# Routed experts block by block, their shares multiplied into y, and the output formed by accumulating transfers

## What is computed

```python
x = x + xattn(_layernorm(x), ctx_1024, Wq, bq, Wk, bk)     # x: (4, 256, 256)
x = x + ffn(_layernorm(x), gate_w, w_gate, w_up, w_down, sh_gate, sh_up, sh_down, se_gate_w)

# xattn: softmax((ctx Wq^T + bq)(ctx Wk^T + bk)^T), applied over the sequence to the normalised x
# ffn, for 1024 tokens, 8 experts, top 2:
scores = xf @ gate_w.T
ew, ei = jax.lax.top_k(scores, 2)
ew = jax.nn.softmax(ew, axis=-1)
x1 = jax.nn.silu(jnp.einsum('td,ehd->teh', xf, w_gate))    # hidden width 128
x3 = jnp.einsum('td,ehd->teh', xf, w_up)
expert_out = jnp.einsum('teh,edh->ted', x1 * x3, w_down)
routed = jnp.einsum('te,ted->td', comb, expert_out)        # comb: ew on the two chosen experts
shared = jax.nn.silu(xf @ sh_gate.T) * (xf @ sh_up.T) @ sh_down.T
sgate = jax.nn.sigmoid(xf @ se_gate_w.T)
return routed + sgate * shared
```

## Time and profile before

| What | Value |
|---|---|
| median of 3 runs | 107.85 us (105.22 to 108.12) |
| the profiled execution's own time | 105.32 us |
| its span, first to last instruction | 103.5 us |
| PE busy | 85.5 us, 83% |
| DVE busy | 62.1 us, 60% |
| ACT busy | 46.5 us, 45% |
| POOL busy | 44.8 us, 43% |
| moved by transfers | 17.50 MB, mean 169 GB/s |

### The profile page before, as it was taken

The page is one execution under the profiler, slowest core; times in us unless marked ns, Lnnn a source line. Parts: engine busy times, 40 slices in busy tenths (PEclk is TensorE's granted clock), DMA queues, the critical chain, the costliest instruction groups (busy, mean ns, idle before and its releaser), DMA issues.

```text
span 103.5 us, 1864 instructions
## 1 busy us (share of the span) xinstructions
PE 85.5 (83%) x514; PEld 68.5 (66%) x514; DVE 62.1 (60%) x274; ACT 46.5 (45%) x104; POOL 44.8 (43%) x60
## 2 busy tenths in 40 slices
PE   6799999997999999996799999999999989600000
PEld 2386789895974478443789999999999968400000
DVE  1188989999999889202986444566444320604990
ACT  0556657758685991433036454466454361000000
POOL 7012002388676777300000567668667677710000
PEclk9999999999999999999999999999999999985555
DMA  2975999992232222256163434655412212059946
GB/s 20 376 267 133 410 413 401 333 348 77 93 108 104 104 104 104 104 142 177 26 186 104 112 107 134 188 152 161 154 46 100 96 56 101 0 90 355 369 180 225
DMA packets 10586, 17.50 MB, mean 169 GB/s; under 512 B 1613, under 2 KB 6095, under 8 KB 10576
## 3 DMA queue, kind: packets, MB, share of 16 engines
q1 hardware_dynamic: 7264, 10.63, 32.7%
q0 software_dynamic: 1872, 4.27, 11.2%
q10 hardware_dynamic: 1440, 2.49, 6.6%
HBM read 10.85 MB, written 7.44 MB: 177 GB/s over the span
## 4 chain that ended last, share of the span: by engine, by line
PE 64%; DMA 12%; DVE 12%; issue 3%; DVEq 3%; POOLq 1%; POOL 1%; ACT 1%; ACTq 0%
PE bank L1064 20%; PE bank L998 12%; PE bank L1079 9%; DMA upper_y<-routed_dram 6%; PE bank L1048 4%; DMA proj_sb<-proj 4%; PE bank L942 4%; PE bank L1034 4%; PE bank L898 3%; PE bank L923 3%; DVEq L285 2%; DMA routed_dram<-y_sb,place 2%; PE bank L906 2%; DVE x L642 2%; PE bank L907 2%
## 5 line engine op out<-in xcount | busy, mean ns | idle before, releaser
L365 POOL DMA_INDIRECT routed_dram<-y_sb,place x23 | 23.6, 1025 | 25.0 <-DVE place L780 15.4
L1064 PEld LDWEIGHTS bank<-xgT,hidden_w 128*128 128x128 f32 x184 | 22.4, 192 | 2.3 <-issue 1.8
L1064 PE MATMUL bank<-xgT,hidden_w 128*128 128x128 f32 x184 | 22.6, 275 | 1.1 <-DVE hidden_w L798 1.1
L352 POOL DMA_INDIRECT slots_dram<-rows,slot x16 | 15.7, 981 | 6.8 <-issue 4.4
L998 PE MATMUL bank<-xnT,ffn_sb 128*128 128x512 f32 (+1 forms) x36 | 14.6, 550 | 0.0
L806 DVE TENSOR_TENSOR r_act<-bank,r_silu 128x256 f32<-128x256 f32 (+1 forms) x12 | 5.0, 414 | 15.9 <-ACT r_silu L514 14.2
L1079 PE MATMUL bank<-ffn_sb,r_act 128*128 x46 | 12.0, 382 | 0.3 <-ACT y_sb L526 0.3
L514 ACT ACTIVATE r_silu<-bank 128x256 f32<-128x256 f32 (+1 forms) x12 | 4.5, 376 | 15.3 <-PE bank L1064 15.3
L998 PEld LDWEIGHTS bank<-xnT,ffn_sb 128*128 128x128 f32 x36 | 6.6, 190 | 5.5 <-issue 5.3
L798 DVE COPY hidden_w<-ffn_sb 128x512 f32 x23 | 8.7, 419 | 1.9 <-issue 1.9
L1079 PEld LDWEIGHTS bank<-ffn_sb,r_act 128*128 128x128 f32 x46 | 7.8, 190 | 1.2 <-issue 0.7
(11 more groups left out here) (119 smaller groups left out, 128.9 us busy)
## 6 DMA issues: line engine op xcount, KB each, us to landing
ffn_sb<-ffn SPq DMA_DIRECT2D x2, 1536.0 KB, 9.6
xg<-slots_dram SPq DMA_DIRECT2D x23, 132.0 KB, 2.2
slots_dram<-empty SPq DMA_DIRECT2D x1, 1056.0 KB, 14.2
x_sb<-x ACTq DMA_DIRECT2D x4, 256.0 KB, 5.0
ffn_sb<-ffn SPq DMA_DIRECT2D x1, 768.0 KB, 4.3
lower_y<-routed_dram SPq DMA_DIRECT2D x2, 256.0 KB, 4.2
lower_y<-routed_dram ACTq DMA_DIRECT2D x2, 256.0 KB, 4.5
upper_y<-routed_dram SPq DMA_DIRECT2D x2, 256.0 KB, 5.6
```

Of the source, the lines that this page charges most:

```text
L352: pool.indirect_dma_start(out=slots_dram[:, :], out_offset=bass.IndirectOffsetOnAxis(ap=slot[:, i, a:a + 1], axis=0), in_=rows[:, i, :], i ...
L365: pool.indirect_dma_start(out=routed_dram[0:planes * TOKENS, :], out_offset=bass.IndirectOffsetOnAxis(ap=place[:, j:j + 1], axis=0), in_=y ...
L1064: last = pe.matmul(hidden_of(p, kind)[:, j % 2, :], hidden_w[:, j % NW, c:c + P], xgT[:, p % 2, k, j % 2, :], start=(k == 0), stop=(k == K ...
```

## The change

The routed stage goes over the 23 blocks one by one: every function takes a block number j, each buffer holds one block, and each semaphore counts blocks. The banks of PSUM are dealt out anew. In DVE's list `experts()` and the first weight copies stand ahead of `shared_act(1, 0)`; in PE's list `shared_up(1, 0)` stands ahead of `shared_gate(1, 1)`.

Two more columns of a table row carry the token's first expert (L + 2) and its negated, scaled margin (L + 3); DVE writes them in `slots`. In the routed stage a DVE instruction makes +-0.5 from the expert (`half`), ACT takes the tanh of the margin column (`lean_of`), DVE makes the share (`share_of`), and ACT's copy of y multiplies by it (`store_y`). `routed_dram`, `lower_y`, `upper_y`, `add_lower`/`add_upper` on DVE and the stores by SP and ACT go. POOL's scatters write to the output tensor itself, which has a second plane for the lower experts' rows. At the end POOL issues four accumulating transfers that add the lower plane to `x1`, then four that add `x1` to the upper plane in DRAM; the first of each wait for the scatters that they need and for `base(1)`.

```diff
-NY = 3
+NY = 6
-LOWS = 4
-UPS = 4
+PARTS = 4
...
-        SH_OUT = [[bank[6], bank[3]], [bank[7], bank[2]]]
+        SH_OUT = [[bank[6], bank[3]], [bank[1], bank[3]]]
         XG_BANK = [bank[0], bank[7]]
-        GU_BANK = [bank[1], bank[2]]
-        Y_BANK = [bank[6], bank[3]]
+        GU_BANK = [bank[4], bank[5]]
+        Y_BANK = [bank[6], bank[2]]
...
             for j in range(BLOCKS):
                 if j >= NXG:
-                    sp.wait_ge(xgT_ready, (j - NXG) // 2 + 1)
-                    sp.wait_ge(place_ready, (j - NXG) // 2 + 1)
+                    sp.wait_ge(xgT_ready, j - NXG + 1)
+                    sp.wait_ge(place_ready, j - NXG + 1)
+                    sp.wait_ge(lean_ready, j - NXG + 1)
                 sp.dma_start(xg[:, j % NXG, :], slots_dram[bass.ds(first[j], P), :]).then_inc(xg_in[j % NXG], 16)
...
             def send_y(j):
...
+                pool.wait_ge(y_stored, j + 1)
+                pool.wait_ge(place_ready, j + 1)
                 planes = 1 if j == LAST else 2
                 pool.indirect_dma_start(
-                    out=routed_dram[0:planes * TOKENS, :],
...
+                    out=planes_of[0:planes * TOKENS, :],
...
+            def add_lower(k):
+
+                t = tiles_of(k)
+                pool.dma_start(x1[:, t, :], out_tiles(1, t), accum_op=ALU.add).then_inc(lower_added[k], 16)
+
+            def add_to_out(k):
+
+                t = tiles_of(k)
+                pool.wait_ge(lower_added[k], 16)
+                pool.dma_start(out_tiles(0, t), x1[:, t, :], accum_op=ALU.add).then_inc(out_stored, 16)
...
             for j in range(BLOCKS):
                 send_y(j)
+            for i in range(NY):
+                mine = [j for j in range(LAST) if j % NY == i]
+                pool.wait_ge(y_sent[i], 16 * len(mine))
+            pool.wait_ge(base_ready, HALVES)
+            for k in range(PARTS):
+                add_lower(k)
+            pool.wait_ge(y_sent[LAST % NY], 16 * rows_sent(LAST % NY))
+            for k in range(PARTS):
+                add_to_out(k)
...
+            def store_y(j):
+                act.wait_ge(y_ready, j + 1)
+                if j >= NY:
+                    act.wait_ge(y_sent[j % NY], 16 * (j // NY))
+                act.wait_ge(share_ready, j + 1)
+                act.activation(y_sb[:, j % NY, :], y_of(j), ACT.Copy, scale=share[:, j:j + 1]).then_inc(y_stored, 1)
+
+            def lean_of(j):
+                act.wait_ge(half_ready, j + 1)
+                act.activation(lean[:, j:j + 1], xg[:, j % NXG, L + 3:L + 4], ACT.Tanh,
+                               scale=half[:, j:j + 1]).then_inc(lean_ready, 1)
...
+            for j in range(BLOCKS):
+                routed_silu(j)
+                if j + 2 < BLOCKS:
+                    store_xgT(j + 2)
+                lean_of(j)
+                if j >= 1:
+                    store_y(j - 1)
+            store_y(BLOCKS - 1)
...
             def slots(b):
                 both = slice(b * LT, (b + 1) * LT)
+
+                dve.tensor_copy(rows[:, both, L + 2], topi[:, both, 0])
+                for i in range(b * LT, (b + 1) * LT):
+                    dve.scalar_tensor_tensor(rows[:, i, L + 3:L + 4], top[:, i, 1:2], top[:, i, 0:1], rstd2[:, i:i + 1],
+                                             ALU.subtract, ALU.mult)
                 dve.wait_ge(prefix_ready, b + 1)
...
+            def places(j):
+
+                dve.wait_ge(xg_in[j % NXG], 16 * (j // NXG + 1))
+                dve.tensor_scalar(plane[:, j:j + 1], xg[:, j % NXG, L + 1:L + 2], expert[:, j:j + 1], float(TOKENS),
+                                  ALU.is_equal, ALU.mult).then_inc(plane_ready, 1)
+
+                dve.tensor_scalar(half[:, j:j + 1], xg[:, j % NXG, L + 2:L + 3], expert[:, j:j + 1], 0.5,
+                                  ALU.not_equal, ALU.subtract).then_inc(half_ready, 1)
+                dve.wait_ge(plane_ready, j + 1)
+                dve.tensor_tensor(place[:, j:j + 1], plane[:, j:j + 1], xg[:, j % NXG, L:L + 1].bitcast(I32),
+                                  ALU.add).then_inc(place_ready, 1)
+
+            def share_of(j):
+                dve.wait_ge(lean_ready, j + 1)
+                dve.tensor_scalar(share[:, j:j + 1], lean[:, j:j + 1], 0.5, 0.5, ALU.mult,
+                                  ALU.add).then_inc(share_ready, 1)
...
             base(0)
-            shared_act(1, 0)
             experts()
             stage(0)
+            stage(1)
+            shared_act(1, 0)
+            stage(2)
             places(0)
...
+            for j in range(BLOCKS):
+                routed_act(j)
+                if j + 3 < BLOCKS:
+                    stage(j + 3)
+                if j == 0:
+                    shared_act(1, 1)
+                share_of(j)
+                if j + 1 < BLOCKS:
+                    places(j + 1)
             base(1)
-            dve.wait_ge(base_ready, 2)
-            for i in range(NT):
-                add_lower(i)
-            for i in range(NT):
-                add_upper(i)
...
             shared_gate(1, 0)
+            shared_up(1, 0)
             shared_gate(1, 1)
-            shared_up(1, 0)
...
+            for j in range(BLOCKS):
+                routed_hidden(j)
+                if j + 2 < BLOCKS:
+                    gather_T(j + 2)
+                if j == 0:
+                    shared_up(1, 1, [1])
                 else:
-                    routed_down(p - 1)
-            routed_down(PAIRS - 1)
+                    routed_down(j - 1)
+            routed_down(BLOCKS - 1)
             shared_down(1, 0)
             shared_down(1, 1)
```

More of the change, by code:

```diff
@@ L46, with xattn_moe_kernel @@
 AX = mybir.AxisListType
[L49 removed]
+def xattn_moe_kernel(nc, proj, x, ffn, slots_dram, out):
     with ExitStack() as ctx:
@@ L131, in xattn_moe_kernel @@
         plane = sb("plane", [P, JB])
+        half = sb("half", [P, JB])
+        lean = sb("lean", [P, JB])
+        share = sb("share", [P, JB])
         place = sb("place", [P, JB], I32)
@@ L150, in xattn_moe_kernel @@
         xg_in = [sem(f"xg_in{i}") for i in range(NXG)]
-        lower_in = [sem(f"lower_in{i}") for i in range(LOWS)]
-        upper_in = [sem(f"upper_in{i}") for i in range(UPS)]
-        lower_added = sem("lower_added")
+        lower_added = [sem(f"lower_added{i}") for i in range(PARTS)]
         warm_ready, ident_ready, const_ready = sem("warm_ready"), sem("ident_ready"), sem("const_ready")
@@ L244, in rows_sent @@
+        def y_of(j):
+            return Y_BANK[j % 2][:, 0:L]
         def rows_sent(i):
-            return sum(blocks_in(p) for p in range(PAIRS) if p % NY == i)
+            return sum(1 for j in range(BLOCKS) if j % NY == i)
         LAST = BLOCKS - 1
[L252 to L272, removed]
@@ L516, in store_y, with store_xgT @@
-            def store_y(p):
-                if p >= NY:
-                    mine = [q for q in range(p) if q % NY == p % NY]
-                    act.wait_ge(y_sent[p % NY], 16 * sum(blocks_in(q) for q in mine))
-                if p < SINGLE:
-                    act.wait_ge(y_ready, 2 * p + 2)
-                    act.copy(y_sb[:, p % NY, :, :], tiles(Y_BANK[p % 2])).then_inc(y_stored, 2)
-                else:
-                    for j in range(2 * p, 2 * p + blocks_in(p)):
-                        act.wait_ge(y_ready, j + 1)
-                        act.copy(y_sb[:, p % NY, j % 2, :], y_of(j)).then_inc(y_stored, 1)
+            def store_xgT(j):
+                act.wait_ge(xgT_ready, j + 1)
+                if j >= 2:
+                    act.wait_ge(gu_ready, j - 1)
+                act.copy(xgT[:, j % 2], XG_BANK[j % 2][:, 0:KT * P].rearrange(
+                    "p (k n) -> p k n", k=KT)).then_inc(xgT_stored, 1)
@@ L1086, in _, with routed_down @@
+            def routed_down(j):
+                if j < 2:
+                    pe.wait_ge(base_ready, 1)
+                else:
+                    pe.wait_ge(y_stored, j - 1)
+                pe.wait_ge(r_act_ready, j + 1)
+                u = bass.ds(chosen[j], 1)
+                pe.matmul(y_of(j), r_act[:, j % 2, :], ffn_sb[:, u, 2 * L:3 * L].rearrange("p o n -> p (o n)"),
+                          start=True, stop=True).then_inc(y_ready, 1)
             pe.wait_ge(warm_ready, 1)
```

238 lines of the change are left out of this document (58 added, 180 removed).

## The result

The changed kernel takes 110.81 us (median of 4 runs, 110.03 to 112.48), the kernel before in the same comparison 106.55 us (median of 4, 105.22 to 108.12): a ratio of 1.051, 95% interval 1.044 to 1.058. The ratio takes only the executions in the faster of the two states in which one and the same kernel can run, 110.03, 110.72 and 110.91 us against 105.22 and 105.25. The forecast was 106.3 us, 1.4% faster than before; the measured time lies within the stated range (102.6 to 111.5), but on the other side of no change, so the forecast was wrong.

What follows compares the result with a forecast made beforehand. PE was taken to bound the routed stage. `base(1)` at 88.7, first issue 89.46, seven more at 1.29 and a landing of 3.5 gave 102.0 against 103.5, so 106.3 us on the median; range 102.6 to 111.5.

Steps and rivals of the forecast that it cites:

- Start of the routed stage: Ahead of the first hidden matmul: the earlier register load and weight copies bring it 1.8 us forward, bounds 0 and 2.1.
- batch 0's stand on the chain, the others' are off it: New DVE instructions in `slots(b)`: 0.25 us for each batch, but only the first batch's lie on the chain of waits.
- Inside the stage: Routed blocks: PE stays at 1.545 us a block, ACT at most 1.45, DVE 1.44; the queue of scatters goes.
- The hand-overs rival: Routed stage: another 0.15 us a round on ACT or DVE makes 3.5 us, in all 110; chance 0.08.
- The tail: After `base(1)`: eight accumulating POOL transfers from 89.46, the eighth issued at 98.5, the end at 102.0, 1.5 us less.
- POOL's pace decides: Transfers at the end: POOL's 1.29 us per issue, not release by landings, sets the eighth issue at 98.5.
- Landing in 3.5, bounds 2.9 to 4.5: Transfers at the end: 2.5 us as for a scatter, plus about 1 us for 256 KB more of reading.
- a sign of being wrong: Transfers at the end: landing needs much over 4.4 us, so that each phase waits for the other's data.
- The rule set against the change: Transfers at the end: adding runs at half a copy's rate, about 10.5 us for 2 MB, an end near 102.
- POOL's queue becomes the bound: Transfers at the end: twice the descriptors, 2.28 us per issue, 5.4 us more, 113.4; chance 0.17.
- Cheap issue: Transfers at the end: POOL issues 0.8 us apart, the second term costs nothing, 5.1 us less, 102.7; chance 0.18.
- The tables: ACT in the routed stage: tanh evicts silu's table, two loads a block, some 50 us more; chance 0.01.

Runs made afterwards that it cites:

- the pair without pauses: Profiles on one chip of the kernel before (105.23 us) and of a3_plain_tail (102.83 us).
- f_no_columns: The changed kernel without DVE's writes of the two new columns, so all shares are a half: 117.71 us, 1.054 of before.
- the run with more slack: a3_plain_tail with the product for y two rounds behind instead of one and a third buffer for `r_act`: 103.71 us, 0.982 of before.
- a3_plain_tail: The changed kernel with the loads by SP and ACT, DVE's adds and the stores of before: 102.83 us against 105.69, ratio 0.974.
- c_copies_on_pool: The changed kernel with POOL's eight accumulating transfers as plain copies, without the adding: 113.14 us, 1.016 of before.

## Why the prediction was wrong, step by step

**Start of the routed stage: right in kind, two thirds of the size.** Forecast was 1.8 us net; it came 49.85 - (51.20 - 2.54) = 1.2 us earlier, and 1.4 in the pair without pauses. The register load does follow `base(0)`, and PE's wait ahead of the first hidden matmul fell from 1.13 us to 0.24. The step that was mis-sized is "batch 0's stand on the chain, the others' are off it": the chain shows 0.08 + 0.25 = 0.33 us in each of three batches, 1.0 us where 0.25 was allowed, and `f_no_columns` confirms it for two of them. In the pair without pauses the shared expert's 16 matmuls ahead of the stage start 37.95 - 37.18 = 0.77 us later, 0.5 more than the 0.25 allowed, which is about what is missing (0.4 to 0.6).

**Inside the stage: right.** Rounds of 1.54 us; scatters no longer queued, the last at 89.55 - 2.54 = 87.0 (86.62 in the pair; forecast 85.7, with 0.4 to 0.6 of the difference from the start). The followers fit: y's copy with the share takes 0.467 us (bound 0.59), the tanh 0.296 (forecast 0.21), with silu 0.278 and xgT's copy 0.373 in all 1.41 for 1.45. Stage by blocks 36.91 us, by pairs 36.27: 0.44 of the 0.64 are two blocks' transposes, which by pairs stood ahead of the stage, and PE's idle time is 0.46 instead of 0.29. That is why the end of `base(1)` moved by only 90.49 - (92.49 - 2.54) = 0.54 us, not 1.8: 1.2 from the start less 0.64. The hand-overs rival did not come; DVE was busy for 22.5 us in the stage, 0.98 a block, where the forecast had up to 1.44.

**The tail: wrong, and the whole of the loss.** The steps that failed are the landing of an accumulating transfer among others and the drain at the end, which the sum did not have. In us behind the end of `base(1)`:

| | Forecast | Measured |
|---|---|---|
| first issue | 0.8 | 0.7 |
| eighth issue | 9.8 | 10.3 |
| last landing | 13.3 | 16.0 |
| end of the program | 13.3 | 18.2 |

The eighth issue came out right for a wrong reason. "POOL's pace decides" failed: an issue costs 0.85 to 0.96 us, not 1.29, and the issues of the second half wait for landings. "Landing in 3.5, bounds 2.9 to 4.5" failed next: the last took 5.76. It priced the adding by what a transfer alone adds to a scatter, and that is nearly right for one alone (3.9 measured), but eight went through full engines at 160 to 198 GB/s. The forecast had named this as a sign of being wrong, a landing of much over 4.4 us with each phase waiting for the other's data, and so it came. The third failure is no term in the sum at all: the program ends with POOL's drain, 2.2 us after the last landing with the final semaphores.

Against the forecast the end lies 6.15 us too late (108.15 for 102.0): 1.25 are the end of `base(1)`, 0.45 the eighth issue, 2.25 its landing and 2.2 the drain. Against before the sum closes too: the end of `base(1)` 0.54 us earlier, the tail 18.20 - 13.04 = 5.16 longer, 4.6 us in all; the spans differ by 108.15 - 103.53 = 4.6. Of the tail, 6.05 us are the adding (by the run without it, 12.15), so that without it the tail would have been 0.9 shorter than the 13.04 before.

**The rule set against the change** held in these profiles. The engines needed 2.1 times as long for the adding transfers as for copies of the same bytes; half of 410 GB/s is 205, and the full engines moved 160 to 198. This is the Trainium skill's "Collectives: The Full Stack" (The bandwidth ceiling), where an adding transfer runs at half a copy's rate. The estimate from it gave an end near 102 from a first issue at 89.46. From the measured one, 93.14, it would give 105.7 for the last landing, which came at 108.5, as the engines moved less at either end (145 GB/s from 95 to 97 us, 162 from 105 to 107). The drain is not in it. That it comes from a second read through one ring, the reason that the Trainium skill gives, no run here shows.

**The rivals.** "POOL's queue becomes the bound" had the right side and its mechanism was refuted: the issue distance that it needed was over 1.51 us, and issues took 0.9. Cheap issue was right in its distance, 0.8, and wrong that the second term costs nothing. The tables were not evicted: tanh beside silu in every round took 0.296 us.

**What stays open.** What POOL's drain waits for is not known. On the two chips with pauses the stage by blocks took 40.1 to 43.4 us in seven profiles, by pairs 36.7, 38.0, 38.0 and 41.3. Whether blocks, with less slack per hand-over, suffer more from a pause, or these profiles caught more of them, was not settled: the run with more slack went where there are none. It matters for the version with the old tail, which gains 2.6% on one chip, while on the two others it can't be told from before (0.995 and 0.997).

## What to carry to other kernels

Before a final add is moved into accumulating transfers, price it at half a copy's rate with several in flight, against the adds of an idle engine: here (`a3_plain_tail`) DVE did the 16 adds in 5.5 us beside loads at twice the rate. Look at who issues the program's last transfer; if it is POOL, add 2 us. Split a change that has several parts before judging it: the finer blocks, the shares in y and the new order are worth 2.6% together where nothing pauses, which the tail more than ate.

## What the runs showed of the hardware

- An accumulating transfer of 256 KB lands 3.9 us after its issue when alone, and in 5.4 to 6.4 us (medians) with others in flight; the engines are then full at 160 to 198 GB/s, beside 410 for plain loads. Eight of them occupied all 16 engines for 13.0 us, plain copies of the same bytes for 6.1.
- POOL issues such a transfer in 0.85 to 0.96 us, a plain one in 0.55 to 0.6, an indirect one in 0.98.
- POOL's drain at the end of the program ended 1.8 to 2.0 us after SP saw POOL's last transfer land, with adding and with plain transfers, and 4.1 us after it where POOL had waited for the landing first.
- PE's pair of matmuls L846 at 5.65 us took 0.85 us in the profile of the changed kernel, and 0.43 in `c_copies_on_pool` and in the same pair before, while the column of granted clocks read 1.00 for 5 to 10 us in the profiles of both kernels.
